# A graph network on one core: layer 2's residual product x·Ws + bs moved from the attention stage to the stage before it

## What is computed

```
h = relu(layernorm(x));  x = x + segment_sum((h @ W0)[src] * w, dst) + b0              # layer 0
h = relu(layernorm(x));  x = x + h + z_in[indeg] + z_out[outdeg] + sigmoid(..) + sigmoid(..)
                              + segment_sum(edge_attr @ W_sum + b_sum, src)               # layer 1
h = relu(layernorm(x))                                                                  # layer 2
q, k, v = h @ wq + bq, h @ wk + bk, h @ wv + bv
attn    = softmax over the edges of one dst of (q[dst] . k[src]) / 16 + w * we + be
out     = segment_sum(v[src] * attn, dst)
y       = layer_norm(h + out + (h @ ws + bs), g1, b1)      # h @ ws + bs: the residual ("own") product
x       = x + layer_norm(y + ffn(y), g2, b2)
```

## Time and profile before

| | us |
|---|---|
| median of 3 runs (lowest, highest) | 6561.62 (6552.72, 6567.17) |
| the profiled execution's own time | 6493.18 |
| its span, first to last instruction | 6491.3 |
| busy in the span: PE, DVE, POOL, ACT | 3748.7, 3726.5, 3566.5, 1497.9 |
| mean granted TensorE clock | 0.869 |

### The profile page before, as it was taken

How to read it: one execution, slowest core, us unless ns; L and a number is a source line. 1 busy time by engine, 2 the same in 40 slices (tenths; PEclk the granted TensorE clock), 3 DMA queues, 4 the chain that set the end, 5 groups by cost and what they waited for, 6 DMA issues and landing times. The chain is left out here.

```text
span 6491.3 us, 98841 instructions
## 1 busy us (share of the span) xinstructions
PE 3748.7 (58%) x15612; PEld 2738.6 (42%) x15613; DVE 3726.5 (57%) x12964; ACT 1497.9 (23%) x5078; POOL 3566.5 (55%) x3854
## 2 busy tenths in 40 slices
PE   0000020005677777777687777777778767777776
PEld 0000010004455555555466566656667634444444
DVE  5249691005566666666566565656655655555565
ACT  1000000000011111111455555555555400111010
POOL 4640686765566666666444444444443666666664
PEclk9999999998777888878788888888889888898888
DMA  4320234454444544445333333333331233333332
GB/s 117 89 70 0 69 84 88 109 162 122 116 133 131 140 132 136 136 131 130 105 104 106 97 98 100 95 100 99 98 100 54 88 90 93 93 92 94 93 92 74
DMA packets 525813, 658.90 MB, mean 102 GB/s; under 512 B 86929, under 2 KB 401822, under 8 KB 525472
## 3 DMA queue, kind: packets, MB, share of 16 engines
q0 software_dynamic: 150160, 395.04, 21.4%
q1 hardware_dynamic: 375441, 261.87, 14.9%
HBM read 550.09 MB, written 106.48 MB: 101 GB/s over the span
## 5 line engine op out<-in xcount | busy, mean ns | idle before, releaser
L1477 POOL DMA_INDIRECT a_row<-h_rows,a_idx x832 | 809.0, 972 | 852.1 <-ACT a_idx L1498 361.2
L2099 POOL DMA_INDIRECT r_row<-h_rows,r_idx x832 | 801.5, 963 | 499.1 <-PE r_p_s L2140 248.9
L465 POOL DMA_INDIRECT src_records<-rec,pos_slot x784 | 809.5, 1032 | 410.0 <-issue 253.6
L993 POOL DMA_INDIRECT s_row<-h_rows,s_rec x832 | 806.9, 970 | 273.5 <-issue 244.5
L1028 PE MATMUL s_sums<-s_row,s_hotw 128*128 128x256 f32 x1664 | 661.2, 485 | 480.0 <-DVE s_hotw L1214 253.1
L1580 PE MATMUL a_p_q<-nodes,a_hotT 128*128 x1664 | 640.1, 472 | 344.1 <-DVE a_score L1681 251.8
L2140 PE MATMUL r_p_s<-r_row,r_hot 128*128 128x272 f32 x1664 | 630.6, 492 | 357.1 <-DVE r_row L2276 202.2
L1222 DVE TENSOR_TENSOR nodes<-nodes,s_sums 128x385 f32 x832 | 455.9, 548 | 521.4 <-remote 278.9
L1681 DVE CUSTOM_DVE_ANT_0 a_prod<-a_p_q,a_row 128x258 f32<-128x258 f32 x832 | 351.3, 422 | 500.3 <-DMA s_rec<-src_records 229.1
L1607 PE MATMUL a_p_s<-a_row,a_masked 128*128 128x257 f32 x1664 | 585.0, 438 | 76.1 <-issue 60.2
L2140 PEld LDWEIGHTS r_p_s<-r_row,r_hot 128*128 128x128 f32 x1664 | 345.8, 230 | 660.9 <-issue 293.1
(11 more groups left out here) (321 smaller groups left out, 7685.9 us busy)
## 6 DMA issues: line engine op xcount, KB each, us to landing
s_rec<-src_records SPq DMA_DIRECT2D x832, 66.0 KB
a_locs<-dloc_rows SPq DMA_DIRECT2D x208, 256.0 KB
rec<-in_edge_attr SPq DMA_DIRECT2D x98, 448.0 KB
s_row<-h_rows,s_rec POOLq DMA_INDIRECT x832
a_row<-h_rows,a_idx POOLq DMA_INDIRECT x832, 2.9
r_row<-h_rows,r_idx POOLq DMA_INDIRECT x832
src_records<-rec,pos_slot POOLq DMA_INDIRECT x784
x_rows<-X SPq DMA_DIRECT2D x1, 6272.0 KB
```

The source lines that it names most:

```text
L465: gp.indirect_dma_start(out=src_records, out_offset=bass.IndirectOffsetOnAxis(ap=pos_slot[:, k:k + 1], axis=0), in_=rec[:, k, :], in_offse ...
L993: gp.indirect_dma_start(out=row[:, k % R, :], out_offset=None, in_=env["h0_rows"], in_offset=bass.IndirectOffsetOnAxis(ap=rec[:, k % R, DS ...
L1477: gp.indirect_dma_start(out=row[:, k, 0:D], out_offset=None, in_=env["h2_rows"], in_offset=bass.IndirectOffsetOnAxis(ap=idx[:, k:k + 1], a ...
L2099: gp.indirect_dma_start(out=row[:, k % R, 0:D], out_offset=None, in_=env["h3_rows"], in_offset=bass.IndirectOffsetOnAxis(ap=idx[:, k:k + 1 ...
```

## The change

The own product with its bias moves from the attention stage into the sources' stage, where the transposed h of the block already lies in SBUF, and h + h·ws + bs is stored as one table `own_rows`. PE gets a node step `project_own` at position 46: one product of ones with bs and two with ws, into the first half of `p_g`. DVE gets `add_own` at 47 + 2, listed ahead of `make_q`, and loses `add_bs`. SP stores one table where it stored two. In the attention stage the own product and the second load go, the value product starts the accumulation itself, and its positions and those behind it move forward by two. Steps that are not named in the diff keep their text; their line numbers shift (L1101 becomes L1099, L1320 becomes L1326, L1293 becomes L1301, L1631 becomes L1623).

```diff
 sources_and_layers_0_1:
-    ADD_BS = 40
-    LOAD_X, STORE, STORE_T = 0, 40, 44
+    OWN, OWN_SUM = 46, 47
+    LOAD_X, STORE, STORE_OWN = 0, 40, 49
...
-                def store_turned(q, k, first):
+                def store_own(q, k, first):
                     b = ranked(q, SP_E)
-                    sp.wait_ge(S["h2_copied"], q + 1)
-                    sp.dma_start(rows_view(env["h2_turned"], b), turned_h[:]...).then_inc(h2t_stored, 16)
+                    sp.wait_ge(S["own_ready"], q + 1)
+                    sp.dma_start(rows_view(env["own_rows"], b), own[:]...).then_inc(own_stored, 16)
...
 gate_arguments (PE):
+                    if not (isinstance(q, int) and q < 3):
+                        pe.wait_ge(S["own_ready"], q - 2)
...
+                def project_own(q, k, first):
+                    pe.wait_ge(S["h2_copied"], q + 1)
+                    pe.wait_ge(S["gates_ready"], min(q + 3, BLOCKS) if isinstance(q, int) else q + 3)
+                    if not first:
+                        pe.wait_ge(S["own_ready"], q)
+                    nc.tensor.matmul(p_g[:, 0:D], c["ones"][0:1, :], bs[:], start=True, stop=False)
+                    for j in range(DC):
+                        last = nc.tensor.matmul(p_g[:, 0:D], turned_h[:, j, :], ws[:, j, :], start=False, stop=j == DC - 1)
+                    last.then_inc(S["own_projected"], 1)
...
-                             (QK, h2_times_qk), (TURN_H, turn_h2)])
+                             (OWN, project_own), (QK, h2_times_qk), (TURN_H, turn_h2)])
...
 norm_x2 (ACT):
-                        ac.wait_ge(S["h2_bs_ready"], q)
+                        ac.wait_ge(S["own_ready"], q)
 copy_h2 (ACT):
-                        ac.wait_ge(h2t_stored, q * 16)
+                        ac.wait_ge(S["own_projected"], q)
...
-                def add_bs(q, k, first):
-                    ve.wait_ge(S["h2_ready"], q + 1)
...
-                    nc.vector.tensor_tensor(h2_bs[:], h2[:], bs[:], ALU.add).then_inc(S["h2_bs_ready"], 1)
+                def add_own(q, k, first):
+                    ve.wait_ge(S["own_projected"], q + 1)
+                    if not first:
+                        ve.wait_ge(own_stored, q * 16)
+                    nc.vector.tensor_tensor(own[:], p_g[:, 0:D], h2[:], ALU.add).then_inc(S["own_ready"], 1)
...
-                          (QUERY, make_q), (ADD_BS, add_bs), (SHIFT2, shift(1)), (EPS2, add_eps(1)), ...
+                          (OWN_SUM, add_own), (QUERY, make_q), (SHIFT2, shift(1)), (EPS2, add_eps(1)), ...
 attention:
-    OWN, TURNED, INVERT, STAGE, TURN, COPY, OTHER, RES, BIAS, STAT, AVG, EPSILON, ROOT, CENTRE, Y = \
-        16, 25, 18, 20, 22, 23, 27, 30, 31, 32, 33, 34, 35, 35, 44
+    OWN, INVERT, STAGE, TURN, COPY, VALUE, RES, BIAS, STAT, AVG, EPSILON, ROOT, CENTRE, Y = \
+        16, 18, 20, 22, 23, 25, 28, 29, 30, 31, 32, 33, 33, 42
...
-                    sp.dma_start(hin[k], own_rows(env["h2_bs_rows"], b)).then_inc(h_in[k], 16)
-                    ...
-                    sp.dma_start(hin_t[k], own_rows(env["h2_turned"], b)).then_inc(ht_in[k], 16)
+                    sp.dma_start(hin[k], own_rows(env["own_rows"], b)).then_inc(h_in[k], 16)
...
-                        last = nc.tensor.matmul(p_o, turned[:, j, :], wv[j], start=False, stop=j == DC - 1)
+                        if j == 0:
+                            pe.wait_ge(E["copied"], q + 1)
+                        ...
+                        last = nc.tensor.matmul(p_o, turned[:, j, :], wv[j], start=j == 0, stop=j == DC - 1)
...
-                      nodes=[(TURNED + j, project_own(j)) for j in range(DC)] + [(TURN, turn)]
-                      + [(OTHER + j, project(j)) for j in range(DC)])
+                      nodes=[(TURN, turn)] + [(VALUE + j, project(j)) for j in range(DC)])
```

More of the change, by code:

```diff
@@ L852, in sources_and_layers_0_1 @@
         bsum = sb(ctx, "bsum", [P, D])
-        bs = sb(ctx, "n_bs", [P, D])
-        h2_bs = sb(ctx, "h2_bs", [P, D])
+        bs = sb(ctx, "n_bs", [1, D])
+        ws = sb(ctx, "n_ws", [P, DC, D])
+        own = sb(ctx, "n_own", [P, D])
         gate = sb(ctx, "gate", [3, 2 * D])
@@ L950, in load_weights @@
                     sp.dma_start(bsum[:], line("L1_gnn_b_sum").broadcast_to([P, D])).then_inc(S["loaded"], 16)
-                    sp.dma_start(bs[:], line("L2_gnn_bs").broadcast_to([P, D])).then_inc(S["loaded"], 16)
+                    sp.dma_start(bs[:], line("L2_gnn_bs")).then_inc(S["loaded"], 16)
                 def load_gates():
@@ L1323, in _ @@
                       nodes=[(DVE_LEAD + p, s) for p, s in (
-                          (QUERY, make_q), (ADD_BS, add_bs), (SHIFT2, shift(1)), (EPS2, add_eps(1)), (AVG2, average(1)), (STAT2, statistics(1, "x2_ready")),
+                          (OWN_SUM, add_own), (QUERY, make_q), (SHIFT2, shift(1)), (EPS2, add_eps(1)), (AVG2, average(1)), (STAT2, statistics(1, "x2_ready")),
                           (X2, make_x2), (H1, add_h1), (SHIFT1, shift(0)), (G2, add_gate(1, "gate_added1", "terms_ready")),
@@ L1384, in beside @@
             return query[:, cols[0]:cols[-1] + 1, RW:RW + P]
-        wv, ws = ([beside(DC) for _ in range(DC)] for _ in range(2))
+        wv = [beside(DC) for _ in range(DC)]
         vec = {n: beside(DC) for n in ("bv", "g1", "b1")}
         hin = [beside(DC) for _ in range(2)]
-        hin_t = [beside(DC) for _ in range(2)]
         staged, turned = beside(DC), beside(DC)
@@ L1403, in attention @@
         S = {n: sem("a_" + n) for n in names}
-        E = {n: sem("e_" + n) for n in ("loaded", "floored", "inverted", "weighed", "staged", "turned", "copied", "own_projected", "projected",
+        E = {n: sem("e_" + n) for n in ("loaded", "floored", "inverted", "weighed", "staged", "turned", "copied", "projected",
                                         "res", "biased", "stated", "averaged", "with_eps", "rooted", "centred", "y_ready")}
         h_in = [sem(f"e_h_in{k}") for k in range(2)]
-        ht_in = [sem(f"e_ht_in{k}") for k in range(2)]
-        LOADS = 2 * DC + len(vec)
+        LOADS = DC + len(vec)
         def ranked(q, engine):
@@ L1450, in load_own @@
                         sp.wait_ge(E["res"], q - 1)
-                    sp.dma_start(hin[k], own_rows(env["h2_bs_rows"], b)).then_inc(h_in[k], 16)
-                    if not (isinstance(q, int) and q < 2):
-                        sp.wait_ge(E["own_projected"], q - 1)
-                    sp.dma_start(hin_t[k], own_rows(env["h2_turned"], b)).then_inc(ht_in[k], 16)
+                    sp.dma_start(hin[k], own_rows(env["own_rows"], b)).then_inc(h_in[k], 16)
                 def load_weights():
-                    for t, n in ((wv, "L2_gnn_wv"), (ws, "L2_gnn_ws")):
-                        for i in range(DC):
-                            sp.dma_start(t[i], own_rows(A[n], i)).then_inc(E["loaded"], 16)
+                    for i in range(DC):
+                        sp.dma_start(wv[i], own_rows(A["L2_gnn_wv"], i)).then_inc(E["loaded"], 16)
                     for n, t in vec.items():
@@ L1607, in sum_rows @@
                     nc.tensor.matmul(p_s[k % 2], masked[:, k % F, :], row[:, k, 0:D + 1], start=True, stop=True).then_inc(S["summed"], 1)
-                def project_own(j):
-                    def step(q, k, first):
-                        if j == 0:
-                            pe.wait_ge(ht_in[k], (q + (2 - k)) * 8)
-                            pe.wait_ge(E["copied"], q + 1)
-                            if first:
-                                pe.wait_ge(E["loaded"], 16 * LOADS)
-                        last = nc.tensor.matmul(p_o, hin_t[k][:, j, :], ws[j], start=j == 0, stop=False)
-                        if j == DC - 1:
-                            last.then_inc(E["own_projected"], 1)
-                    return step
                 def turn(q, k, first):
@@ L1630, in step @@
                     def step(q, k, first):
-                        last = nc.tensor.matmul(p_o, turned[:, j, :], wv[j], start=False, stop=j == DC - 1)
+                        if j == 0:
+                            pe.wait_ge(E["copied"], q + 1)
+                            if first:
+                                pe.wait_ge(E["loaded"], 16 * LOADS)
+                        last = nc.tensor.matmul(p_o, turned[:, j, :], wv[j], start=j == 0, stop=j == DC - 1)
                         if j == DC - 1:
```

25 lines of the change are left out of this document (8 added, 17 removed).

## The result

The changed kernel takes 6621.2 us (median of 4 runs, 6607.9 to 6645.3), the kernel before 6559.3 us (4 runs, 6552.7 to 6567.2) beside it. The ratio is 1.0098, with a 95% interval of 1.0063 to 1.0133: some 62 us slower. The direction was as forecast, the size was nearly twice the +32.

What follows compares the result with a forecast made beforehand. No engine fills either stage; a ring of DVE's `n_vare`, POOL's root and gathers, DVE's additions and `deg` was taken to bound. 31 + 6 - 3 - 1.5 = +32 us on 6561.6 gives 6594 us, range 6545 to 6635.

Steps and rivals of the forecast that it cites:

- The attention, -4.5: Attention stage: PE's earlier hand-over is given back behind POOL's gathers, -3 us; value product starts earlier at the end, -1.5.
- the "faster" rival: Attention: DVE's dot product stops waiting for PE, half the blocks expose it, 36 us won; 6520 us, chance 0.17.
- The sources' stage, +37 in the loop and +6 at its end: Sources' stage: 37 us of DVE delay per-block in sum, 31 reaching the end; unhidden last product, addition and store +6.
- the two blocks before it only in part: End of the sources' stage: the last block's lengthening touches the two preceding blocks only partly; within +6, between +3 and +10.
- A + B: Sources' stage: the new addition's delay of `n_vare` plus DVE's wait for the own product, 37 us over 49 blocks.
- B: Sources' stage: DVE's addition waits 1.1 us for PE's own product at the slow clock, 20 us; bounds 0 and 54.
- A: Sources' stage: `add_own` ahead of `n_vare` delays it 0.34 us in each of 49 blocks, 17 us.
- The factor of 0.85: Sources' stage: share of the 37 us delay reaching the end, taken between 0.62 and 1, giving 31 us.
- Much slower: Sources' stage: PE waits at the own product for the sigmoid, delaying every following sum; 6650 us, chance 0.10.
- No change: Sources' stage: only a third of the delay reaches the end, 37 us becoming 12, end effects nearly cancel; 6565, chance 0.23.
- The port rule: Sources' stage: DVE with two SBUF inputs excludes POOL's SBUF reads; removing `add_bs` would return up to 20 us; not counted.
- `add_bs` given back 0: Sources' stage: removing the old addition gains nothing, as DVE then stands longer; 17 us if the ring ran through it.

Runs made afterwards that it cites:

- the two kernels with the moved loop: Kernel before and changed kernel, each with eight more empty DVE instructions ahead of the attention's loop, eight fewer before the last stage: 6465.8 us (0.9933) and 6490.7 us (0.9965).
- the addition-last kernel: Changed kernel with the new addition put behind `n_vare`, last in DVE's list: 0.9993 of before on the faster chip, 1.0065 on the slower.
- the best version: Changed kernel with eight more empty instructions before the attention's loop, own product at 51, addition at 54, store at 56: 5082.7 us, 0.9759 of before, faster chip only.
- the PE product alone: Kernel before plus only the own product on PE in the sources' stage, read by nobody: 1.0000 and 1.0001 on the faster chip, 0.9992 on the slower.

## Why the prediction was right in sign and half the size

The clearest sum is that of the two kernels with the moved loop, one profile each, where no refetch disturbs: sources' stage +70 (1638.6 to 1708.6), attention -49 (1979.3 to 1930.4), last stage +6.5 (1355.8 to 1362.3), together +27.6, and +24.9 timed. On top of it comes the refetch, which costs the changed kernel 94 us and before 51 (timed), so 43 more. 25 + 43 = 68, the +68 of the changed kernel on that chip; the first pair gave +62. The forecast +32 came near the first of the two parts by luck, through two errors that cancel, and knew nothing of the second. That the total came inside the stated range is owed to that luck.

**The attention, -4.5: this step failed.** The prediction held that what PE hands over earlier DVE gives back behind POOL's gathers, so that taking 72 us of PE's work off the attention is worth 3. The attention became 49 us shorter, which is also past the 15 us that the prediction named as a sign of being wrong. DVE's dot product, first in before with the moved loop (3200 to 4850 us), then in the changed kernel with it (3280 to 4930 us):

```profile
L1681 DVE CUSTOM_DVE_ANT_0 a_prod<-a_p_q,a_row 128x258 f32<-128x258 f32 x795 | 336.3, 423 | 419.9 <-DMA s_rec<-src_records 234.1 <-PE a_p_q L1580 131.0 <-issue 52.9
L1672 DVE CUSTOM_DVE_ANT_0 a_prod<-a_p_q,a_row 128x258 f32<-128x258 f32 x798 | 336.8, 422 | 355.7 <-DMA s_rec<-src_records 172.4 <-PE a_p_q L1580 117.7 <-issue 63.1
```

Its idle time fell by 64 us. 62 of them were put down to a DMA and only 13 to PE, while "issue" grew by 10. So the place is that of the "faster" rival and the gain is larger than the 36 it gave, but its mechanism, that DVE stops waiting for PE, is not shown: PE's busy time fell by only 11 us in this pair (1523.84 to 1512.45, the granted clock going from 0.88 to 0.85), and the second load and the steps' places changed with it. That the rival did not decide the whole is due to the two parts below.

**What took it back, not in the prediction at all:** the change shifts DVE's instructions, and the attention's loop came to lie so that a second wait of 2.8 us on average follows the first instruction of each turn. Before, there was one such wait per turn, now two. DVE's sequencer shows it. In the changed kernel the turn at 4078.67 begins with L151 at 4081.1 us, and the next instruction (L1652) starts at 4083.7. In before these two start at 4061.7 and 4061.8. All 20 turns are alike: the gap between the two instructions is 2.3 to 3.2 us in the changed kernel and 0.12 to 0.14 us in before and in both moved kernels. That the refetch costs time is shown by the two moved kernels. That the second wait is due to a boundary of the fetched pieces right behind the loop's first instruction is my reading of the trace, not tested by a third placement. The Trainium skill (Runtime: NRT & Kernel Launch, section Instruction fetch mechanics) says that a jump to a page outside the window of two forces a fetch before execution goes on; the traces agree, with 4.24 and 6.62 us at the jump. It speaks of blocks of 16 KiB, while this queue's packets are of 8 KB (0.04 MB in 5); whether two of them make a block no run here shows.

**The sources' stage, +37 in the loop and +6 at its end: mis-sized, and part of it missing.** Over the profiles on slower chips it is 1630 us with the old step (1624.0, 1638.6, 1627.6) and 1708 with the new (1694.5, 1721.1, 1708.6): +78. The time from the stage's last gather to the attention's first is 45.8 to 47.3 us before and 57.1 to 61.2 after, about +12 in place of +6. The timeline of the changed kernel at the end:

```profile
3179.07 1.22 PE L1107 MATMUL p_g<-n_bs,ones 1*128 1x256 f32 x2
...
3180.21 2.08 PE L1109 MATMUL p_g<-n_ws,turned_h 128*128 128x256 f32 x4
3182.33 0.42 DVE L1318 TENSOR_TENSOR n_own<-p_g,h 128x256 f32<-128x256 f32 x1 [7.12 <-PE p_g L1109]
...
3182.93 0.33 SPq L976 DMA_DIRECT2D own_rows<-n_own  x1
3186.12 0.36 SPq L1435 DMA_DIRECT2D a_web<-in_L_gnn_we  x1
```

The product takes 3.2 us, as costed. The step of the end that was short is "the two blocks before it only in part": DVE waited 2.19 and 3.91 us there too, 13.2 us for three own products where before it had waited 4.3 us for three key products.

Within the loop, 66 us remain. The mean time between the starts of DVE's additions (`nodes<-nodes,s_sums`) in the interval that holds the new step rose from 1.6 us to 2.3, 2.7 and 2.7 in the three profiles: 0.6 to 1.0 us in each of 49 blocks, 31 to 51 us, where A + B was 37. The timeline shows one block with the wait at the slow clock, PE's product ending at 2033.10:

```profile
2031.03 2.07 PE L1109 MATMUL p_g<-n_ws,turned_h 128*128 128x256 f32 x4
...
2033.23 0.42 DVE L1318 TENSOR_TENSOR n_own<-p_g,h 128x256 f32<-128x256 f32 x1 [1.88 <-PE p_g L1109]
...
2034.57 0.14 DVE L1301 TENSOR_SCALAR n_vare<-n_mv 128x1 f32<-128x1 f32 x1
...
2034.92 0.56 POOL L1009 TENSOR_TENSOR n_rstd<-n_vare,n_half 128x1 f32<-128x1 f32 x1 [1.63 <-DVE n_vare L1301]
```

In this block it is the chain as forecast, link by link. DVE's waits for the product in the whole stage are 27.8 us in 12 places here, 44.5 and 38.8 us in 21 in the two other profiles; 13 to 17 us of each lie in the tail, which leaves 15 to 28 us in the loop, where B was 20. With A = 17 that is 32 to 45 us, near the 31 to 51 seen. So A + B has the right size in DVE's own interval. That it reaches the stage's length through `n_vare` is only in part supported: with the addition behind `n_vare` the same interval is still 2.3 us, POOL's wait mostly moves to `deg`, and the timed gain of 27 us is likely but not settled. The factor of 0.85 was low if it counts waiting roots: 79 of 81 wait. The other 15 to 35 us of the 66 were not in the prediction and stay open. The new wait of `xv` is no answer: it is 44.8 us in this profile and 13.2 in that of the moved loop, and both stages grew alike.

**The rivals.** Much slower (PE waiting for the sigmoid): refuted, in the groups PE's new step has at most 5.4 us of idle time over 41 blocks, and PE's product added alone costs nothing. No change: by its own terms (12 + 6 - 4.5) it came to 6575, not to 6565, which is the lower end of the forecast case. Faster: not what happened at this placement; on the faster chip the version with moved loop and later product is faster. The port rule was not tested by itself.

**`add_bs` given back 0**: no run isolates it. On the faster chip moving that addition was worth -9 us.

**What stays open:** the 15 to 35 us named above; what the waits of SP and PE on the new addition cost; what in the attention gave the 49 us; the +12 us in the last stage on average (1352.9 to 1364.8), which the change doesn't touch; which stage gave the addition-last kernel its better time; and whether the best version wins as much on the slower chip. It was not run there. The changed kernel itself was not run on the faster chip.

## What to carry to other kernels

Before costing a change in a kernel with loops, look at the instruction queue's packets and at the "issue" gap of an engine's first instruction in each turn: here eight empty instructions were worth 51 and 94 us, more than the change under study. When a change moves work between stages, judge both sides by runs with that effect taken out, since a sum that comes out near can hide a +70 and a -49. And that a view puts an engine's waits down to a DMA does not say that work taken off another engine is worth little: the attention lost 72 us of PE's work and one load per block and became 49 us shorter, although DVE's waits had mostly been put down to a DMA.

## What the runs showed of the hardware

The attention's loop on DVE is refetched every turn, 5 packets of 8 KB and 3.3 or 5.3 us of standing, in before and in the changed kernel, and not at all with eight more empty instructions ahead of it: whether it is depends on where the loop lies. Chips differ by a quarter on identical kernels (5212 to 5217 against 6517 to 6559 us). A gather takes 0.97 us on both and DVE's dot product 0.42. The granted clock of the sources' stage is 0.80 to 0.83 on the slower and 0.91 to 0.97 on the faster. The clock alone isn't the reason: the work ahead of the sources' stage takes 1489 us on the slower (before) and 1205 on the faster (the PE product alone, the same there) at a granted clock of 1.00 on both, with the same busy time of PE (60.9) and POOL (839 and 838). On the slower chip POOL waits for DVE at most roots, on the faster at almost none, and the own product costs 78 us of the sources' stage on one and, at its later place, nothing on the other. What makes the chips differ is open.
